# Layer norm's means and variances of seven chunk pairs, moved from round 19 to rounds 17 and 18 of a pipelined recurrence

## The reference, cut to what matters

```python
x = x + L0_attn(lstm_a(x))                 # recurrence a, then linear attention
x = x + L0_ffn(rnn_c(x))                   # recurrence c, then experts
h = lstm_e(x)                              # recurrence e, layer 1's first LSTM
mu = jnp.mean(h, axis=-1, keepdims=True)
var = jnp.mean(jnp.square(h - mu), axis=-1, keepdims=True)
hn = (h - mu) * jax.lax.rsqrt(var + 1e-5) * gamma + beta
q, k, v = hn @ Wq + bq, hn @ Wk + bk, hn @ Wv + bv
...
```

## Time and profile before

| | us |
|---|---|
| median of three runs | 2752.63 |
| the three runs | 2752.63, 2743.34, 2756.63 |
| the profiled execution's own time | 2752.09 |
| its span, first to last instruction | 2750.3 |
| slots 303 to 322 of it | 90.2 |
| mean granted TensorE clock | 0.945 of full speed |

### The profile page before, as it was taken

The page is one execution under the profiler, slowest core; times in us unless marked ns, Lnnn a source line. Parts: engine busy times, 40 slices in busy tenths (PEclk is TensorE's granted clock), DMA queues, the critical chain, the costliest instruction groups (busy, mean ns, idle before and its releaser), DMA issues. The chain is left out here.

```text
span 2750.3 us, 119322 instructions
## 1 busy us (share of the span) xinstructions
PE 2431.2 (88%) x50848; PEld 2034.0 (74%) x50848; DVE 1921.9 (70%) x7392; ACT 1155.6 (42%) x3690; POOL 419.4 (15%) x412
## 2 busy tenths in 40 slices
PE   1678999999999999987858858999999999999999
PEld 0455677777777777654536648999999999999998
DVE  4567877777777777788666646767767776766664
ACT  3124555555555555556336723333333333333333
POOL 0000000000000000000009911222222222222222
PEclk9678999999999999999759958999999999999999
DMA  5000000000000000010013330000000000000000
GB/s 169 1 2 3 5 5 5 5 5 5 5 5 5 5 5 5 6 42 27 4 43 89 93 93 22 9 9 9 9 9 9 9 9 9 9 9 9 5 5 6
DMA packets 52747, 53.66 MB, mean 20 GB/s; under 512 B 24934, under 2 KB 46840, under 8 KB 50042
## 3 DMA queue, kind: packets, MB, share of 16 engines
q1 hardware_dynamic: 46868, 26.81, 3.6%
q0 software_dynamic: 2000, 14.68, 1.6%
q10 hardware_dynamic: 3350, 4.54, 0.5%
HBM read 39.46 MB, written 6.55 MB: 17 GB/s over the span
## 5 line engine op out<-in xcount | busy, mean ns | idle before, releaser
L105 PE MATMUL p<-xn,m_h 128*128 128x128 f16 x6144 | 557.5, 219 | 0.0
L105 PE MATMUL p<-xn,m_l 128*128 128x128 f16 x3072 | 528.8, 219 | 0.0
L105 PEld LDWEIGHTS p<-xn,m_h 128*128 128x128 f16 x6144 | 479.9, 98 | 1.8
L2047 POOL TENSOR_TENSOR xn<-qkv_w,xn 128x384 f16<-128x384 f32 x256 | 233.9, 914 | 908.6 <-ACT xn L2005 908.6
L576 PE MATMUL lg_b<-xn,lh 128*32 128x256 f16 x6144 | 297.8, 289 | 79.4 <-DVE lh L1016 77.8
L992 DVE STREAM_TRANSPOSE gt<-lg_b 128x512 f32<-128x512 f32 x324 | 230.2, 710 | 188.0 <-PE lg_b L576 187.5
L814 ACT ACTIVATE gl<-gt 128x128 f32<-128x128 f32 x324 | 100.3, 309 | 601.9 <-DVE gt L992 601.4
L829 ACT ACTIVATE hm<-xy,b 128x512 f32<-128x512 f32 x512 | 348.0, 680 | 0.1
L105 PEld LDWEIGHTS p<-xn,m_l 128*128 128x128 f16 x3072 | 300.6, 98 | 0.7
L1931 PE MATMUL po<-m_h,xn 128*128 128x256 f16 x1536 | 292.6, 272 | 1.9 <-DVE xn L2086 1.9
L576 PEld LDWEIGHTS lg_b<-xn,lh 128*32 128x32 f16 x6144 | 158.5, 101 | 164.1 <-DVE lh L1016 129.3
(11 more groups left out here) (385 smaller groups left out, 6218.9 us busy)
## 6 DMA issues: line engine op xcount, KB each, us to landing
m_stage<-in_m_w POOLq DMA_DIRECT2D x12, 1024.0 KB, 6.0
hs<-in_m_w SPq DMA_DIRECT2D x14, 384.0 KB, 3.2
xs<-in_x POOLq DMA_DIRECT2D x1, 2048.0 KB, 8.4
x_dram<-x SPq DMA_DIRECT2D x16, 128.0 KB, 2.1
xs<-in_l_wv SPq DMA_DIRECT2D x1, 2048.0 KB
attention_dram<-att SPq DMA_DIRECT2D x16, 128.0 KB, 2.9
xn<-x_dram SPq DMA_DIRECT2D x16, 128.0 KB, 2.5
out_dram<-xn SPq DMA_DIRECT2D x16, 128.0 KB, 2.2
```

Source lines behind the costliest of these rows:

```text
L105: ins = pe.matmul(out, w[wp](k), x[xp](k), start=start, stop=last and k == KT - 1 and xp == 1, skip_group_check=True)
L2047: pool.tensor_tensor(a_l[:, n % 2, :], a32[:, n % 2, :], a_h[:, n % 2, :], ALU.subtract).then_inc(a_lo, 1)
```

## The change

The units 0 to 6 move from the slots 303 to 309, one in each, to the slots 282, 285, 288, 291, 294, 297 and 300. Their means are written to `c_bank`, which is the recurrence c's bank g_c under a new name, with the variances' sums in 16 columns behind it (`vars_`); before, means were in xy[0] and sums in xy[1]. The wait for the last `gelu` becomes one for the last step of recurrence c. The squares go to one buffer in `nd`'s place, where there were two (in `tmp` and `gs`), so that a square waits for the sum of the unit before. The root moves from slot 311 to slot 302, the single unit 7 stays in slot 311 (ROOT + 9), the pairs 0 to 6 move to the slots 305, 307, 310, 312, 315, 317 and 320, and `norm_spread` writes to xy[0] and waits for the last `gelu`. No instruction is added or removed.

```diff
-        NORM = (NCH + 2) * C + C - 1
+        NORM = (NCH + 1) * C + C0 + 1
-        UNIT_AT = {NORM + u: u for u in range(NPAIR - 1)} | {NORM + NPAIR: NPAIR - 1}
-        ROOT = NORM + NPAIR
-        PAIR_AT = {ROOT + 2 + 3 * p // 2: p for p in range(NPAIR - 1)}
+        ROOT = (NCH + 2) * C + C - 2
+        UNIT_AT = {NORM + 3 * u: u for u in range(NPAIR - 1)} | {ROOT + 9: NPAIR - 1}
+        PAIR_AT = {ROOT + 3 + 5 * p // 2: p for p in range(NPAIR - 1)}
-        sq = [tmp[:, :, :, :].rearrange("p u k n -> p (u k n)").rearrange("p (k n) -> p k n", k=KT),
-              gs[:, :, :, :].rearrange("p u k n -> p (u k n)").rearrange("p (k n) -> p k n", k=KT)]
+        sq = nd[:, :, :, :].rearrange("p k u n -> p k (u n)")
-        g_c = ctx.enter_context(nc.psum_tensor("g_c", [P, C, KT, B], F32))
+        c_bank = ctx.enter_context(nc.psum_tensor("c_bank", [P, 512], F32))
+        g_c = c_bank[:, 0:KT * CW].rearrange("p (s k b) -> p s k b", k=KT, b=B)
+        vars_ = c_bank[:, KT * CW:KT * CW + NCH]
...
             def norm_mean(u):
-                pe.wait_ge(g_32, 2 * N_E)
+                pe.wait_ge(c_32, NCH * C)
-                    last = pe.matmul(xy[0][:, 0:n * CW], mean_w[:, :], xn(c, n)[:, k, :], start=(k == 0),
+                    last = pe.matmul(c_bank[:, 0:n * CW], mean_w[:, :], xn(c, n)[:, k, :], start=(k == 0),
...
             def norm_spread(p):
-                pe.wait_ge(c_32, NCH * C)
+                pe.wait_ge(g_32, 2 * N_E)
-                pe.matmul(g_c[:, :, :, :].rearrange("p s k b -> p (s k b)"), mean_w[:, :], diag[p % 2], start=True,
+                pe.matmul(xy[0][:, 0:PAIR], mean_w[:, :], diag[p % 2], start=True,
...
             def norm_square(u):
-                if u >= 2:
-                    act.wait_ge(n_var, u - 1)
-                act.activation(sq[u % 2][:, :, 0:n * CW], xn(c, n), ACT.Square).then_inc(n_sq, 1)
+                if u >= 1:
+                    act.wait_ge(n_var, u)
+                act.activation(sq[:, :, 0:n * CW], xn(c, n), ACT.Square).then_inc(n_sq, 1)
```

More of the change, by code:

```diff
@@ L766, in norm_var @@
                     for k in range(KT):
-                        last = pe.matmul(xy[1][:, c + j:c + j + 1], sq[u % 2][:, k, j * CW:(j + 1) * CW],
+                        last = pe.matmul(vars_[:, c + j:c + j + 1], sq[:, k, j * CW:(j + 1) * CW],
                                          mean_w[:, 0:1], start=(c + j == 0 and k == 0), stop=(k == KT - 1),
@@ L923, in norm_sqrt @@
                 act.wait_ge(n_var, (NPAIR - 1, NPAIR + 1)[r])
-                act.activation(va[:, a:b], xy[1][:, a:b], ACT.Relu, bias=eps[:, :]).then_inc(n_va, 1)
+                act.activation(va[:, a:b], vars_[:, a:b], ACT.Relu, bias=eps[:, :]).then_inc(n_va, 1)
                 act.wait_ge(n_va, r + 1)
@@ L1198, in norm_center @@
                 dve.wait_ge(n_mean, u + 1)
-                dve.tensor_tensor(xn(c, n), xn(c, n), xy[0][:, 0:n * CW].unsqueeze(1).to_broadcast([P, KT, n * CW]),
+                dve.tensor_tensor(xn(c, n), xn(c, n), c_bank[:, 0:n * CW].unsqueeze(1).to_broadcast([P, KT, n * CW]),
                                   ALU.subtract).then_inc(n_d, 1)
@@ L1238, in norm_scale @@
                                              scalar=gscale[:, k:k + 1],
-                                             in1=g_c[:, :, :, :].rearrange("p s k b -> p (s k b)"), op0=ALU.mult,
+                                             in1=xy[0][:, 0:PAIR], op0=ALU.mult,
                                              op1=ALU.mult).then_inc(n_x, 1)
```

## The result

| | before | after |
|---|---|---|
| median of 20 runs each | 2746.4 us (2741.9 to 2762.0) | 2759.2 us (2755.6 to 2765.5) |
| mean of the same runs | 2748.7 us | 2760.0 us |
| profiled execution, own time | 2752.1 us | 2761.8 us |

The ratio of after to before is 1.0043, with an interval of 1.0032 to 1.0054: some 12 us more. The forecast was 2756.5 us (4.2 more than a base of 2752.1 to 2752.6), in a range of 2744 to 2767. So the time lies in the range and the change within 0.5%; the sign is right, and the size is not: +12 where +4 was forecast. The interval leaves out 1, so these runs do tell the slowdown from no change.

The account below looks back on a forecast made before the run. The prediction took the recurrence's loop through the engines, about 3.05 us a slot, to bound the kernel. Its terms, 11.3 + 2.4 + 2.0 - 11.5 = +4.2 us, gave 2756.5 us, range 2744 to 2767.

Parts of the forecast that it names:

- The mean slots: Slots 282, 285 to 300: state 1.55 us later in each of seven, projection extra in 291 and 294; +11.3 us.
- The variance slots: Slots behind the mean slots: recurrence starts later, +0.47 us in 292, 295 and 301; +2.4 us in all.
- The clock in rounds 17 and 18: Slots 282 to 302: one or two short falls of PE's clock, 2 us in all.
- rival 1: Slots 282 to 302: clock falls; all 21 slots at half clock cost 26 us instead of 2, so 2781; chance 0.11.
- The single buffer, ACT's square and the bank: Moved units in rounds 17 and 18: one squares buffer, ACT's later square and the shared bank cost 0.
- The root: Slot 302: ACT's table loads for the square root, behind a spread copy, make the gates late; 1.4 us.
- Slot 323: Slot 323: no `norm_low` holds up its state any more; 0.9 us less.
- The tail: Slots 303 to 322 shrink from 90.2 to 79.6 us (10.6 less), plus 0.9 in slot 323; -11.5 us together.
- Rival 2: Tail, after the change: keeps the full clock, 10.7 us less, so 2746; chance 0.04.
- The base: Whole kernel: time before the change, profiled execution 2752.1 us or median 2752.63, to which +4.2 us was added.
- No change that can be told: Whole kernel: change within about 0.5% (13.8 us), taken as what a measurement can tell; chance 0.84.

Follow-up runs that it names:

- experiment 2: Changed kernel with DVE's centring called behind the new state instead of ahead of it: 2754.8 us, ratio to the kernel before 1.0012.
- Experiment 3: Changed kernel with PE's variance and mean called before `w2`, the centring still ahead of the state: 2757.1 us, ratio to the kernel before 1.0037.
- experiment 1: Kernel before with only the change's banks (means and variances' sums in recurrence c's bank, spread in `xy[0]`): 2745.9 us, ratio 0.9995.
- experiment 8: Changed kernel, centring behind state, variance and mean before `w2`, unread tail matmuls: 2744.4 us; last kernel, also units two slots apart from 288: 2740.5 us.
- experiment 6: Unread matmuls added in PE's idle tail time to hold the clock: kernel before 2743.6 us, ratio 0.9971; changed kernel 2755.5 us, ratio 1.0012.
- experiment 4: Changed kernel with centring behind the state and variance and mean before `w2`: 2754.3 us, ratio to the kernel before 1.0016.

## Why the prediction was right or wrong, point by point

- **The mean slots (11.3 us): right.** The plain ones grew by 1.60 (288, 297, 300), 291 and 294 by 1.80, for 1.55 and 1.79. Experiments 2 and 3 show both halves of the cause, the centring ahead of the state and the mean behind `w2`. Slot 282 was missed: it holds a projection of e too (another 0.2), and in the changed kernel it grew by 2.32. Its recurrence's last group of matmuls is broken by 0.28 us in which PE waited for nothing that the profile shows, and the next transpose comes 1.34 us after the first matmul, where it is 0.89 in slot 297; why is open.
- **The variance slots (2.4): right, a little low.** 0.50 to 0.57 for 292, 295 and 301, 0.78 in 298, 0.61 in 286 (0.25 forecast), 0 in 283 and 289: 3.0 in all. Experiment 3 took the 0.5 away.
- **The clock in rounds 17 and 18 (2.0): too large by half.** One fall, on slot 285, which grew by 2.64 instead of 1.60: 1.0 us. The sum of 15.7 came out near the measured 16.4 because slot 282 and the variances made up for it, which is luck. Nor is a fall there wholly the change's: the traces of experiment 1 and of the kernel before with its clock held have 6.8 us at half clock there too, and their stretch is 1.2 us longer than in the profiled execution. Of rival 1 there is only this one fall.
- **The single buffer, ACT's square and the bank, at nothing: right** (experiment 1 for the bank, the last kernel of experiment 8 for the buffer; the other mean slots have no excess that is left over).
- **The root (1.4): too small.** In slot 303 the gates are 1.6 us late, and the whole slot costs 2.4 us more than the one without the root (5.66 against 3.23). The remaining 0.8 is not split here; DVE's five small operations on the root stand ahead of the next transpose.
- **Slot 323 (-0.9): right.** From its transpose to the state DVE took 2.69 us before and takes 1.91: -0.8.
- **The tail (-11.5): the step that failed, as a size.** I took 90.2 us "from the transpose of slot 303 to that of slot 323" as what the tail costs before. For the profiled execution that is right, and so was the difference to it, -10.0 for -10.6. But the run times say that about half of the executions of before don't have that tail. In the one shown it is 81.9, and then the change gives back only 1.7. As an estimate, with -10.0 in one half and -1.7 in the other the gain is about 6, and +16.4 less 6 is some 10 us, near the 11.3 by which the means differ. An allowance for a second clock pattern would have moved the sum to about +9. The -10.0 itself came out of two misses that cancel in part: the root cost 1.0 more than forecast, and less of the tail was at half clock than the 17 of 20 slots that I took (mean granted clock 0.67, where 0.55 was to show).
- **Rival 2, the tail at full clock, did not come** by itself: 52.5 of 80.2 us are at half clock. The Trainium skill ("TensorE: Matmul & The Clock Gate", section "Why this matters for your kernels") wants the gaps between bursts short to keep the clock. The tail of before doesn't agree that this is enough: from slot 303 to the fall at 1343.1 PE was never idle for more than 1.7 us at a time. For the changed kernel the prediction was wrong to call the gaps short: they reach 4.5 us, and one of 3.79 lies right ahead of the tail's first fall, at 1356.1, so that its tail doesn't speak against the rule. Filling the idle time did hold the clock for the most part (experiment 6).
- **The base.** The profiled execution at 2752.1 lies in the upper group. The median of the three runs, 2752.6, agreed with it by chance; the median of 20 is 2746.4. That the time of 2759.2 came within 3 us of the forecast is luck in part: the base was 6 us too high and the change 8 to 9 us too small.
- **"No change that can be told": only by the limit chosen.** The change of 0.43% is under the 0.5% that the prediction set, but 20 runs each gave an interval of 0.32 to 0.54%, so 0.5% was too coarse for what such a measurement tells.

What stays open: why the stretches without changed work differ by up to 6 us between traces, and so why experiments 3 and 4 gave back less in time than in their slots; and what decides early or late which way the tail's clock goes in the kernel before.

## What to carry to other kernels

Where a stretch's cost rests on a clock that falls, one profile prices only one of its patterns: take more than one execution before you book the stretch as a gain, and look for two groups in the run times. A loop that passes through every engine has no idle time for work placed in its queue ahead of the state it hands on; what looks empty on PE must be put before what it waits for, not behind it, and DVE's part behind the state. And work that is free at full clock (the variance ahead of `w2` in slots 295 and 301) may cost 3 us in a slot over which the clock has fallen (286).

## What the runs showed of the hardware that was not expected

- One program showed two patterns of the granted clock in the same stretch, in four profiled executions: full to 1343.1 and then half to 1384.1 (three of them nearly so), or half from 1337.0 to 1340.4 and then full to 1364.3 (one). They are 8.3 us apart over 20 slots, and about 10 in the run times.
- In the first pattern the clock fell at 1343.1 though PE had not been idle for more than 1.7 us at a time since slot 303 began.
- More work on PE made a kernel faster and its times closer: 76 matmuls of 512 columns in the tail (0.38 us each) took its half-clock time from 70.2 us (48.1 in the other pattern) to 3.4, and the runs' spread from some 20 us to 6, at a ratio of 0.9971 (0.9953 to 0.9989). The gain is over the slower executions; its median of 2743.6 us is that of the lower group.
- A unit's variance, recorded as eight f32 matmuls of one column each, takes 1.05 us at full clock and 1.87 at half.
- A switch of ACT's function table and back cost 1.28 us each way and no more: from the start of the first load at 1351.68 to the gates at 1354.50 are 2.82 us, with an activation of 0.21 between.
